# High-part products first on TensorE, and layer 2's bias additions held on GpSimd until the aj columns exist

## What is computed

```python
# layer 0: a small group GCN on the first 25 nodes
# layer 1: attention
z = x @ W.T + bW;  ai = z @ wai + bai;  aj = z @ waj + baj
e = leaky(ai + aj.T);  att = where(adj > 0, e, -9e15)
f1 = softmax([att, -1e9])[:, :n] @ z
# layer 2
h = (1 + eps) * x + adj @ x
f2 = relu(h @ W1 + b1) @ W2 + b2
# layer 3
agg = eps * x + adj @ x
f3 = silu(rmsnorm(agg @ W1 + b1) * w) @ W2 + b2
```

## Time and profile before

| | |
|---|---|
| median of 3 runs | 2935.29 us (2935.02 to 2937.99) |
| the profiled execution, own time | 2933.81 us |
| its span, first to last instruction | 2932.0 us |
| its instructions | 41513 |
| mean granted TensorE clock | 0.973 |
| busy: PE, DVE, ACT, POOL | 93%, 77%, 49%, 45% |

### The profile page before, as it was taken

One profiled execution on the slowest core, in us unless ns is written; L12 is line 12 of the kernel. 1 busy time (PEld: TensorE's weight loads), 2 busy tenths in 40 slices (PEclk: granted clock), 3 DMA queues, 4 the chain that ended last, 5 costly groups with the idle time before them and its releaser, 6 DMA issues.

```text
span 2932.0 us, 41513 instructions
## 1 busy us (share of the span) xinstructions
PE 2720.4 (93%) x14794; PEld 2292.7 (78%) x14794; DVE 2271.9 (77%) x4709; ACT 1433.9 (49%) x2772; POOL 1316.1 (45%) x1392
## 2 busy tenths in 40 slices
PE   3819999999999999999999999999999999999997
PEld 3707787888878787887878788887878788787886
DVE  3265889797878879787887979788887979788734
ACT  0223463746455473646456374645547364544624
POOL 1103455444535544454545544463554435454442
PEclk8958999999999999999999999999999999999999
DMA  4024031120404022030403112040402203040200
...
DMA packets 205502, 181.06 MB, mean 62 GB/s; under 512 B 17617, under 2 KB 186993, under 8 KB 205297
## 3 DMA queue, kind: packets, MB, share of 16 engines
...
## 4 chain that ended last, share of the span: by engine, by line
PE 41%; DVE 38%; ACT 6%; issue 6%; POOL 2%; DMA 1%; SPq 0%; DVEq 0%; POOLq 0%; ACTq 0%
PE bank L795 12%; PE bank L820 8%; DVE stat L1304 5%; PE bank L755 5%; PE bank L757 4%; PE bank L756 4%; DVE att L1355 4%; DVE att L1360 4%; PE bank L706 3%; DVE sq_sum L1327 3%; DVE x_even L1319 3%; DVE x_odd L1319 3%; DVE mt_lo L1262 2%; DVE scratch L1343 2%; POOL rstd L1136 2%
## 5 line engine op out<-in xcount | busy, mean ns | idle before, releaser
L755 PE MATMUL bank<-mt_hi,x_hi 128*128 128x512 f32 x1536 | 639.7, 416 | 1.8
L757 PE MATMUL bank<-mt_hi,x_lo 128*128 128x512 f32 x1536 | 606.5, 395 | 0.0
L756 PE MATMUL bank<-mt_lo,x_hi 128*128 128x512 f32 x1536 | 604.6, 394 | 0.0
L1136 POOL TENSOR_TENSOR rstd<-ve,neg_half 128x4 f32<-128x4 f32 x128 | 147.6, 1153 | 499.3 <-DVE ve L1312 499.3
L755 PEld LDWEIGHTS bank<-mt_hi,x_hi 128*128 128x128 f32 x1536 | 291.9, 190 | 77.9 <-POOL x_lo L1141 20.9
L757 PEld LDWEIGHTS bank<-mt_hi,x_lo 128*128 128x128 f32 x1536 | 291.0, 189 | 65.4
L1388 DVE TENSOR_TENSOR sq_sum<-sq_sum,scratch 128x512 f32<-128x512 f32 x224 | 154.7, 691 | 232.1 <-ACT scratch L1025 232.1
L756 PEld LDWEIGHTS bank<-mt_lo,x_hi 128*128 128x128 f32 x1536 | 292.7, 191 | 49.5
L795 PE MATMUL bank<-a_hi,W_hi 128*128 128x512 f32 x768 | 319.5, 416 | 11.9 <-DVE a_lo L1276 11.4
L820 PE MATMUL bank<-W_hi,hid_hi 128*128 128x256 f32 x1024 | 294.7, 288 | 24.8 <-DVE hid_lo L1392 19.1
L795 PE MATMUL bank<-a_hi,W_lo 128*128 128x512 f32 x768 | 304.4, 396 | 0.0
...
## 6 DMA issues: line engine op xcount, KB each, us to landing
att<-in_adj SPq DMA_DIRECT2D x128, 512.0 KB, 7.8
adj_col<-in_adj SPq DMA_DIRECT2D x256, 256.0 KB, 3.0
...
```

What stands on the lines that cost most here:

```text
L755: nc.tensor.matmul(dst[:], hi, mt_hi[:, k, cols], start=k == 0, stop=False)
L756: nc.tensor.matmul(dst[:], hi, mt_lo[:, k, cols], start=False, stop=False)
L757: mm = nc.tensor.matmul(dst[:], lo, mt_hi[:, k, cols], start=False, stop=done)
L1136: nc.gpsimd.tensor_tensor(rstd[:, norm, own], ve[:, norm, own], neg_half[:, 0:4], ALU.pow)\
```

## The change

Four things change. In `agg_step`, `x_ready` now waits for the high part of x, and the wait for the low part stands before the third product of the step's first feature block. In `hidden_tile`, the order of the six products is now: low weights by high aggregate and high by high for both feature blocks, and last the two with the low part of the aggregate; at m = 0 each feature block waits for its high part (`a_high`), and the wait `a_ready` has moved from ahead of the tiles to behind the four high products. For m = 0 of half 0 there is a wait ahead of all for the first low part, since the product overwrites the bank from which it is made. In `second_step3`, the eight products with the hidden tile's high part come first and wait for that part alone, and then the four with the low part. On GpSimd, ahead of layer 2's `add_bias` stands a wait for the next graph's aj (not in the last graph), and `diag_gap` of half 1 and both `diag_lo` stand between the additions.

```diff
--- before.py
+++ after.py
@@ -739,7 +739,7 @@
                     pe.wait_ge(s_turn_free[i], use + 1)
 
             def x_ready(b, layer, k):
-                pe.wait_ge(s_x_lo, x_count(b, layer - 1, k))
+                pe.wait_ge(s_x_hi, x_count(b, layer - 1, k))
 
             def agg_step(b, layer, k, h, second_bank=None, ds=range(DT)):
                 cols = slice(h * HALF, (h + 1) * HALF)
@@ -754,6 +754,8 @@
                     done = k == NT - 1
                     nc.tensor.matmul(dst[:], hi, mt_hi[:, k, cols], start=k == 0, stop=False)
                     nc.tensor.matmul(dst[:], hi, mt_lo[:, k, cols], start=False, stop=False)
+                    if d == ds[0]:
+                        pe.wait_ge(s_x_lo, x_count(b, layer - 1, k))
                     mm = nc.tensor.matmul(dst[:], lo, mt_hi[:, k, cols], start=False, stop=done)
                     if done:
                         mm.then_inc(s_agg, 1)
@@ -762,6 +764,9 @@
 
             def a_ready(b, layer, h):
                 pe.wait_ge(s_a_lo, DT * agg_count(b, layer, h))
+
+            def a_high(b, layer, h, d):
+                pe.wait_ge(s_a_hi, DT * agg_count(b, layer, h) - 1 + d)
 
             def out_free(b, layer, h, j):
                 n = 4 * (layer - 1) + 2 * h + j
@@ -790,10 +795,19 @@
                         pe.wait_ge(s_sq, b * 2 * HT3 + i - 1)
                 w_hi, w_lo = (W12_hi, W12_lo) if layer == 2 else (W13_hi, W13_lo)
                 cols = slice(m * P, (m + 1) * P)
+                dst = hid_bank[i % 2][:]
+                if m == 0 and h == 0:
+
+                    pe.wait_ge(s_a_lo, DT * agg_count(b, layer, h) - 1)
                 for d in range(DT):
-                    for n, (l, r) in enumerate(((w_hi, a_hi), (w_hi, a_lo), (w_lo, a_hi))):
-                        mm = nc.tensor.matmul(hid_bank[i % 2][:], l[:, d, cols], r[:, d, :], start=(d == 0 and n == 0),
-                                              stop=(d == DT - 1 and n == 2))
+                    if m == 0:
+                        a_high(b, layer, h, d)
+                    nc.tensor.matmul(dst, w_lo[:, d, cols], a_hi[:, d, :], start=d == 0, stop=False)
+                    nc.tensor.matmul(dst, w_hi[:, d, cols], a_hi[:, d, :], start=False, stop=False)
+                if m == 0:
+                    a_ready(b, layer, h)
+                for d in range(DT):
+                    mm = nc.tensor.matmul(dst, w_hi[:, d, cols], a_lo[:, d, :], start=False, stop=d == DT - 1)
                 mm.then_inc(s_hid_mm, 1)
 
             def second_step2(b, h, m):
@@ -812,14 +826,17 @@
                 if m == 0:
                     for j in range(2):
                         out_free(b, 3, h, j)
-                pe.wait_ge(s_hid_lo[h], b * HT3 + m + 1)
+
+                pe.wait_ge(s_hid_hi[h], b * HT3 + m + 1)
                 hi, lo = hid_hi[:, m % 4, :], hid_lo[:, m, :]
                 for t in HALF_TILES:
-                    cols = slice(t * P, (t + 1) * P)
-                    for n, (l, r) in enumerate(((hi, W23_hi), (hi, W23_lo), (lo, W23_hi))):
-                        mm = nc.tensor.matmul(out_bank[t // 2][:, t % 2 * D:(t % 2 + 1) * D], l[:, cols], r[:, m, :],
-                                              start=(m == 0 and t % 2 == 0 and n == 0),
-                                              stop=(m == HT3 - 1 and t % 2 == 1 and n == 2))
+                    for n, r in enumerate((W23_hi, W23_lo)):
+                        nc.tensor.matmul(out_bank[t // 2][:, t % 2 * D:(t % 2 + 1) * D], hi[:, t * P:(t + 1) * P],
+                                         r[:, m, :], start=(m == 0 and t % 2 == 0 and n == 0), stop=False)
+                pe.wait_ge(s_hid_lo[h], b * HT3 + m + 1)
+                for t in HALF_TILES:
+                    mm = nc.tensor.matmul(out_bank[t // 2][:, t % 2 * D:(t % 2 + 1) * D], lo[:, t * P:(t + 1) * P],
+                                          W23_hi[:, m, :], start=False, stop=(m == HT3 - 1 and t % 2 == 1))
                     if m == HT3 - 1 and t % 2 == 1:
                         mm.then_inc(s_out, 1)
                 if m < HT3 - 1:
@@ -896,7 +913,6 @@
                     if k == 6 and not last:
                         aj_rows(b + 1, False)
                 for h in range(2):
-                    a_ready(b, 2, h)
                     for m in range(HT2):
                         hidden_tile(b, 2, h, m)
                     for m in range(HT2):
@@ -910,7 +926,6 @@
                     agg_step(b, 3, k, 0)
                 for k in range(4, 6):
                     agg_step(b, 3, k, 1)
-                a_ready(b, 3, 0)
                 for m in range(HT3):
                     hidden_tile(b, 3, 0, m)
                     if not last and m in (0, 4):
@@ -925,7 +940,6 @@
                 rms_row(b, 0)
                 if not last:
                     turn_att(b + 1, 3)
-                a_ready(b, 3, 1)
                 for m in range(HT3):
                     hidden_tile(b, 3, 1, m)
                     second_step3(b, 0, m)
@@ -1212,12 +1226,16 @@
                     rstd_of(b + 1, 0, 1)
                 for t in tiles(1):
                     x_low(b, 1, t, buf)
+                if not last:
+
+                    pool.wait_ge(s_aj, b + 2)
                 for t in range(NT):
                     add_bias(b, 1, t, buf)
+                    if t == 0:
+                        diag_gap(b, 1)
+                        diag_lo(b, 0)
                     if t == 3:
-                        diag_gap(b, 1)
-                for h in range(2):
-                    diag_lo(b, h)
+                        diag_lo(b, 1)
                 rstd_of(b, 2, 0)
                 for t in tiles(0):
                     x_low(b, 2, t, buf)
```

## The result

The changed kernel takes 2894.7 us (median of 4 runs, 2891.1 to 2899.57), the kernel before, run beside it, 2936.35 us (4 runs, 2935.02 to 2937.99). The ratio is 0.9859, with a 95% interval of 0.9842 to 0.9876: faster by 41.6 us. A second measurement of the same kernel gave 2896.76 us against 2935.35, a ratio of 0.987 [0.9857, 0.9884] (experiment 11). The forecast was 2889 us, 46 us faster. The profiled execution took 2891.1 us, of which the span is 2889.3, against a span of 2932.0 before: 42.7 us.

The account below looks back on a forecast made before the run. PE's list of work plus its stalls was taken to bound the kernel; 15 graphs of 2.2 + 0.7 us plus 2.5 us in the last make 46 us, hence 2889 us, own bounds 2880 to 2900, range 2867 to 2913.

Parts of the forecast that it names:

- The hold on DVE's side: Attention sums before aj: without POOL beside them aj is done 3.9 us earlier, PE's 2.2 us stall goes, DVE gains 3.1.
- Its price on POOL's side: Layer 2's held additions: 0.2 us for a mask, four collisions with scores 1.3 us; DVE's low parts net 1.6 us earlier.
- High parts first, at half 1: Layer 2's half 1: four products, 0.93 us, run ahead of the low-part wait; PE leaves 2.5 us earlier, still waiting near 1 us.
- So of the 2.5 us PE keeps 2.2 us here: Layer 3's hidden tiles: DVE 1.6 us earlier plus 0.6 us for needing one low part leave PE 2.2 us per graph.
- The second step: Layer 3's second step: starting with `hid_hi`, eight high products cover the rest of the low part; 0.7 us per graph.
- The added waits cost nothing: Some 76 added waits per graph, in the aggregates and elsewhere on PE, cost nothing where they are served.
- The sum: Whole run: 15 graphs at 2.2 + 0.7 us give 43.5, the last graph 2.5, in all 46 us.
- The collisions vanish: Rival, chance 0.16: POOL finishes before the scores, DVE keeps 3.1 us, first term 3.7 us; 2867 us.
- In full: Rival, chance 0.12: each held addition blocks DVE 0.73 us at the scores, DVE's gain is 0; 2913 us.
- Slower: Rival, chance 0.05: all eight additions block in full in three score rows, 5.8 us against 3.1 gained; 2954 us.
- nothing: Rival, chance 0.07: aj is late for another reason and PE stalls at the next place instead; about 2930 us.
- I am wrong if PE stalls anew in front of layer 3: Sign against the forecast: a new PE stall ahead of layer 3 in the changed profile.

Follow-up runs that it names:

- experiment 11: The changed kernel, unaltered, measured once more: 2896.76 us, ratio 0.987.
- Kernel 7: Changed kernel without GpSimd's wait for aj, its new order of additions, gap and diagonals kept: 2917.94 us, ratio 0.9943.
- Kernel 4: Changed kernel plus a second hold: layer 2's last four bias additions wait until the third row of scores is masked; 2872.08 us, ratio 0.9799.
- Kernel 10: Changed kernel with later layer 2 and layer 3 additions held, first `x_low` behind row 3's leaky, second `diag_lo` behind the third masked maximum: 2843.1 us, ratio 0.9686.
- kernel 2: Changed kernel with GpSimd's old list, so PE's high parts first alone, without the hold: 2919.93 us, ratio 0.9949.
- Kernel 8: Changed kernel plus a hold: GpSimd's first `x_low` of layer 3 waits for the leaky of the next graph's row 3; 2884.45 us, ratio 0.9832.
- kernel 3: Kernel before with only `second_step3` of the changed kernel: 2920.97 us, ratio 0.9954.
- kernel 6: Changed kernel with `x_ready` waiting for the low part of x again, no wait inside the aggregation step: 2901.02 us, ratio 0.9891.

## Why the prediction was right

The direction, the mechanism and the size were right, the size by 5.7 us: 2889 us forecast, 2894.7 measured, in the likeliest case's own bounds of 2880 to 2900. Part of this closeness is luck: some 3 us of the gain came with the granted clock in the start-up, and the repetition, at 2896.76 us, lies 8 us from the forecast. Point by point:

- **The hold on DVE's side.** Right. The sums take 0.42 us, aj starts right behind them, PE's 2.2 us are gone (2.44 to 0.22), and the transposes start when PE arrives. Kernel 7 shows that it is the wait and not the new order. The aj columns are done 4.6 us earlier and not 3.9 (from 2.38 us behind the zero to 2.18 ahead of it), since one of the sums had taken 1.40 us; nothing comes of this, because DVE then waits for PE. One reading of the rows doesn't hold: the sum of 0.41 us stands beside GpSimd's additions too (1296.59 against 1295.13 to 1298.47) and not in a cheap spell. No term rests on it.
- **Its price on POOL's side.** Right: four collisions, at rows 1 and 2 of the scores, for 1.3 us (two masks 0.35 and 0.33, a leaky 0.35, a maximum 0.29). The 0.2 us put down for a mask are 0.13, at the first maximum (2.20 to 2.33). The copies start 0.86 us behind the zero instead of 3.90, and 3.04 - 1.32 - 0.13 = 1.6. The low parts of half 1 were to be 1.6 us earlier; they are 1.58 (17.58 to 16.00 behind the zero). Kernel 4, which takes these four collisions away, gets 1.32 us back. Kernel 10 shows a larger one that the prediction passed over since it changes little: the diagonal on the first maximum, 1.1 us, in the kernel before as well.
- **High parts first, at half 1.** The time at this place was right: PE idles 1.27 us in the middle of the tile. (The idle time of 1.48 us before, which the prediction reads from one graph, isn't in every graph: where the clock was low, PE came too late for it.) Its worth was not right: alone it makes DVE 0.7 us later, and the first low part at layer 3, 0.6 us as forecast, only gives this back (kernel 2).
- **"So of the 2.5 us PE keeps 2.2 us here".** This is the step that failed. PE keeps 1.68 us at the hidden tiles of layer 3 (51.75 to 50.07). The sum carried DVE's 1.6 us on to layer 3 unchanged, and 0.5 of them got lost on the way, since PE's earlier tiles, by way of ACT, brought POOL's first `x_low` onto the leaky of row 3. The prediction asked what the held additions would collide with; it didn't ask that of the work that became early. Kernel 8 shows the loss by getting it back, with 0.3 us more from the maximum behind it; the graphs of kernel 2 with a late PE show it too.
- **The second step.** Forecast 0.7 us, measured 0.7 alone (kernel 3), 0.74 in the changed kernel (from the hidden tiles to the second step 22.53 and 21.79 us).
- **The added waits cost nothing.** Nothing contradicts this; kernel 6 shows that the split of the wait for x even earns 0.43 us. The prediction had it in the sum without a price of its own.
- **The sum.** Forecast 2.9 us per graph, measured 2.50 over 14 graphs. The fifteenth and the start-up gave 5.6 + 1.1 us, of which some 3 came with the granted clock, and the 1.1 lie within the spread of the start-up. Behind the last aj transposes 1.0 us was gained, less than I had counted for the last graph.
- **The rivals.** "The collisions vanish" is out: they are at 1.63 and 1.50 us. "In full" is out for these four. "Slower" and "nothing" are out. "I am wrong if PE stalls anew in front of layer 3" came true in the small: 0.6 us at L755, for the high part of x, and 0.2 at L759.
- **The rule weighed.** The four additions of 0.73 us cost DVE 0.33 us each, and took 1.55 us each themselves; the first maximum beside a diagonal of 1.29 us lost 1.1 us. The Trainium skill ("SBUF — State Buffer", section "SBUF: two separate sides") says of such a pair that "the other fully blocks". By that rule, as the prediction worked it out, the additions would have cost up to 2.9 us, for an estimated 2913 us in all. The trace agrees for the diagonal, and it doesn't for the additions.

What stays open: why an addition or subtraction of 128x256 costs DVE 0.3 to 0.5 us where the diagonal costs 1.1; why kernel 10's maxima in rows 4 and 6 (1.50 and 1.51 us) and the leaky of rows 4, 6 and 7 beside `x_low` lose 0.3 us, and not more or less; and whether `x_low` could be placed so that it meets none of them. That wasn't tried.
